# Scores of 16 small heads: four-pass float32 matmuls against halves stacked by DMA for single-pass matmuls

## The reference, cut to what matters

```
def mha(q_in, k_in, v_in, ...):
    Q = (q_in @ qw + qb).reshape(Bq, Lq, 16, 8)
    K = (k_in @ kw + kb).reshape(Bq, Lk, 16, 8)
    V = (v_in @ vw + vb).reshape(Bq, Lk, 16, 8)
    scores = jnp.einsum('bqhd,bkhd->bhqk', Q, K) / np.sqrt(8)
    attn = jax.nn.softmax(scores, axis=-1)
    out = jnp.einsum('bhqk,bkhd->bqhd', attn, V).reshape(Bq, Lq, 128)
    return out @ ow + ob
```

## Time and profile before

| | |
|---|---|
| time, median of 3 | 1052.72 us (1051.87 to 1052.78) |
| span of the profiled execution, first to last instruction | 1049.9 us |
| what lies around that span, against the median | 2.8 us |
| granted TensorE clock, mean over the span | 0.990 |
| TensorE (PE) busy | 1008.1 us, 96% |
| VectorE (DVE) busy | 748.8 us, 71% |
| GpSimd (POOL) busy | 686.9 us, 65% |
| ScalarE (ACT) busy | 607.4 us, 58% |
| DMA queues | 5.9%, 0.6% and 0.1% of 16 engines' span |

### The profile page before, as it was taken

How to read it: one execution, slowest core, us unless ns; L and a number is a source line. 1 busy time by engine, 2 the same in 40 slices (tenths; PEclk the granted TensorE clock), 3 DMA queues, 4 the chain that set the end, 5 groups by cost and what they waited for, 6 DMA issues and landing times.

```text
span 1049.9 us, 28844 instructions
## 1 busy us (share of the span) xinstructions
PE 1008.1 (96%) x11729; PEld 636.9 (61%) x11729; DVE 748.8 (71%) x1852; ACT 607.4 (58%) x898; POOL 686.9 (65%) x819
## 2 busy tenths in 40 slices
PE   7889999999999999999999999999999999999998
PEld 5345555556655776667676655665556566565576
DVE  7778888778884443776787788878888866777421
ACT  2144445577667455455554576776666677766752
POOL 6688988687986332111114699987889777688720
PEclk9699999999999999999999999999999999999999
DMA  6300000000001102000000000000000000000011
GB/s 217 122 2 2 22 12 13 20 14 23 12 22 28 36 31 99 13 7 7 8 7 19 14 8 2 2 2 2 3 1 2 2 2 2 2 2 2 1 41 41
DMA packets 9282, 22.76 MB, mean 22 GB/s; under 512 B 1392, under 2 KB 1648, under 8 KB 8768
## 3 DMA queue, kind: packets, MB, share of 16 engines
q1 hardware_dynamic: 9152, 20.94, 5.9%
HBM read 18.77 MB, written 2.15 MB: 20 GB/s over the span
## 4 chain that ended last, share of the span: by engine, by line
PE 82%; DVE 7%; POOL 5%; issue 4%; ACT 2%; DMA 0%; SPq 0%; POOLq 0%; ACTq 0%; DVEq 0%
PE weighed L708 12%; PE scores L680 11%; PE row_scores L643 7%; PE scores L906 6%; PE weighed L731 5%; PE scores L598 4%; PE quads L579 4%; DVE negmax L1226 3%; PE quads L605 3%; PE scores L693 3%; PE row_scores L906 3%; PE quads L590 3%; PE row_scores L721 2%; PE scores L721 2%; PE weighed L923 2%
## 5 line engine op out<-in xcount | busy, mean ns | idle before, releaser
L1226 DVE TENSOR_REDUCE negmax<-row_scores 128x8 f32<-128x616 f32 (+1 forms) x312 | 298.8, 958 | 100.4 <-PE row_scores L643 74.9
L1731 ACT ACTIVATE p<-scores 128x1024 f32<-128x1024 f32 (+1 forms) x253 | 250.9, 1020 | 165.6 <-PE scores L693 139.2
L680 PE MATMUL scores<-qblk,work 32*77 32x512 f32 (+1 forms) x1256 | 202.8, 612 | 6.2 <-ACT p L1731 3.3
L708 PE MATMUL weighed<-p,v 77*32 77x128 f32 (+1 forms) x5120 | 172.9, 276 | 0.1
L1906 POOL TENSOR_TENSOR qblk<-work,pack_const 128x512 f32<-128x512 f32 x160 | 166.5, 1041 | 0.0
L1916 POOL TENSOR_TENSOR kblk_r<-work,pack_const 128x308 fp32r<-128x308 f32 (+1 forms) x160 | 134.0, 838 | 44.4 <-PE row_scores L643 27.0
L643 PE MATMUL row_scores<-kblk_r,qr 32*128 32x308 f32 (+1 forms) x624 | 140.9, 443 | 13.8 <-DVE negmax L1226 12.3
L708 PEld LDWEIGHTS weighed<-p,v 77*32 77x32 f32 (+1 forms) x5120 | 130.0, 109 | 36.0 <-issue 29.4
L643 PEld LDWEIGHTS row_scores<-kblk_r,qr 32*128 32x128 f32 x624 | 61.4, 185 | 98.0 <-issue 70.9
L693 PE MATMUL scores<-nblk,select 32*77 32x512 bf16 (+1 forms) x628 | 94.8, 376 | 0.0
L1242 DVE STREAM_TRANSPOSE nat<-weighed 128x256 f32<-128x256 f32 x160 | 70.9, 443 | 32.6 <-PE weighed L708 30.7
(11 more groups left out here) (332 smaller groups left out, 1862.9 us busy)
## 6 DMA issues: line engine op xcount, KB each, us to landing
shared<-gates_hbm SPq DMA_DIRECT2D x24, 256.0 KB, 3.1
shared<-in_ctx_tok SPq DMA_DIRECT2D x15, 154.0 KB
pack_w_l<-in_w_l SPq DMA_DIRECT2D x1, 2058.5 KB, 11.5
x<-in_x_tok SPq DMA_DIRECT2D x8, 256.0 KB, 6.2
out_x<-x SPq DMA_DIRECT2D x8, 256.0 KB, 2.0
layers_w<-in_w_l SPq DMA_DIRECT2D x1, 1289.0 KB, 9.8
ctxT<-in_ctxT SPq DMA_DIRECT2D x1, 1232.0 KB, 8.9
layers_w<-in_w_ada SPq DMA_DIRECT2D x1, 582.0 KB, 5.5
```

Source lines behind the costliest of these rows:

```text
L680: mm = e.matmul(score_banks(n, g // 2)[0:nk, g % 2, :], k_of[q % 3][at, s * nk:(s + 1) * nk], qblk[n % 2][at, :], start=layer.mask != "qk" ...
L708: mm = e.matmul(av_bank[TILE * j:TILE * j + TILE, i2 * S:(i2 + 1) * S], v[0:nk, at:at + TILE], p[n % 2][0:nk, g * NJ + j, :], start=i1 == ...
L1226: e.tensor_reduce(negmax[q % 2][:, 2 * h:2 * h + 2, s * NJ:(s + 1) * NJ], row_banks(n, h)[:, :, 0:NJ * nk].rearrange("p g (j k) -> p g j k ...
L1731: e.activation(p[n % 2][0:nk, 8 * h:8 * h + 8, :], score_banks(n, h)[0:nk].rearrange("p g (j q) -> p (g j) q", j=NJ), ACT.Exp, bias=hide, ...
```

## The change

The exact scores are made otherwise. Once a quad, ScalarE rounds the keys too (`round_k`; the queries already were), and GpSimd subtracts the rounded from the exact value (`split_q`, `split_k`), so that queries and keys are there as a high and a low half. SyncE then stacks them for two jobs at a time (`stack_pair`): eight SBUF-to-SBUF DMAs put, for each head, the four products high x high, low key x high query, and so on (`PARTS`), into 32 partitions (8 dims x 4 parts), in rings of three pairs. The weights are permuted on the host (`_by_dim`), so that the heads of a group lie in every fourth partition. `exact` is now 16 matmuls of 32 rows and 128 columns, one for each head, in rounded float32; `qblk` and `spread_q` are gone. The first `exact` of a pair waits for its 8 DMAs. `q_of` and `k_of` are rings of two. In slots with 128 keys `shift(t, 1)` now follows `shift(t, 0)` directly, ahead of `quad_ahead`. SyncE's program is written in slots as well, since the loads of gates and context now stand between the stacking.

```diff
 (exact, TensorE)
-                ready, value = k_ready(q)
-                w.wait_ge(ready, value)
-                w.wait_ge(qblk_done, n + 1)
-                for g in range(NG):
-                    at = slice(TILE * g, TILE * (g + 1))
-                    mm = e.matmul(score_banks(n, g // 2)[0:nk, g % 2, :], k_of[q % 3][at, s * nk:(s + 1) * nk], qblk[n % 2][at, :],
-                                  start=layer.mask != "qk" or g >= 2, stop=False, skip_group_check=True,
-                                  tile_position=(TILE * g, 0))
+                m, half = divmod(n, 2)
+                w.wait_ge(*pair_landed(m))
+                for j in range(NJ):
+                    for g in range(NG):
+                        at = slice(TILE * g, TILE * (g + 1))
+                        mm = e.matmul(score_banks(n, g // 2)[0:nk, g % 2, j * S:(j + 1) * S],
+                                      keys_of(m, nk)[at, j, half * nk:(half + 1) * nk].bitcast(F32R),
+                                      q_ring[m % PAIRS][at, j, half * S:(half + 1) * S].bitcast(F32R),
+                                      start=j == 0 and (layer.mask != "qk" or g >= 2), stop=False, skip_group_check=True,
+                                      tile_position=(TILE * g, 0))
 (attention, TensorE)
                         exact(t)
                         shift(t, 0)
-                        if not is_wide(t):
-                            shift(t, 1)
+                        shift(t, 1)
                     if is_wide(t):
                         quad_ahead(qi, cl)
-                        shift(t, 1)
 (ScalarE)
+            def round_k(q):
+                cols = QUAD * layer_of(q).nk
+                ready, value = k_ready(q)
+                w.wait_ge(ready, value)
+                w.wait_ge(k_split, q)
+                if q:
+                    w.wait_ge(*pair_landed(2 * q - 2))
+                    w.wait_ge(*pair_landed(2 * q - 1))
+                e.copy(k_high[:, 0:cols], k_of[q % 2][:, 0:cols]).then_inc(k_rounded, 1)
...
                         exponentiate(t, 0)
                     if cl == 2 and qi + 1 in quads:
                         round_max(qi + 1)
+                    if cl == 3 and qi + 2 in quads:
+                        round_k(qi + 2)
                     if t in jobs:
                         exponentiate(t, 1)
 (GpSimd)
+            def split_q(q):
+                w.wait_ge(qr_done, q + 1)
+                if q:
+                    w.wait_ge(*pair_landed(2 * q - 2))
+                    w.wait_ge(*pair_landed(2 * q - 1))
+                e.tensor_tensor(q_low, q_of[q % 2], qr[q % 3][:, :].bitcast(F32), ALU.subtract).then_inc(q_split, 1)
...
-                    if t + 1 in jobs:
-                        spread_q(t + 1)
...
+                    if cl == 3 and qi + 2 in quads:
+                        split_q(qi + 2)
+                        split_k(qi + 2)
 (SyncE)
+            def stack_pair(m):
+                q, half = divmod(m, 2)
+                nk = layer_of(q).nk
+                q_at, k_at = (slice(2 * half * n, 2 * (half + 1) * n) for n in (S, nk))
+                w.wait_ge(q_split, q + 1)
+                w.wait_ge(k_split, q + 1)
+                w.wait_ge(scores_done, 2 * (m - PAIRS) + 2)
+                landed = pair_landed(m)[0]
+                for x, (of_q, of_k) in enumerate(PARTS):
+                    k_src = k_low if of_k else k_high[:, :].bitcast(F32)
+                    e.dma_start(keys_of(m, nk)[x:128:NJ, :, :], k_src[:, k_at]).then_inc(landed, 16)
+                for x, (of_q, of_k) in reversed(list(enumerate(PARTS))):
+                    q_src = q_low if of_q else qr[q % 3][:, :].bitcast(F32)
+                    e.dma_start(q_ring[m % PAIRS][x:128:NJ, :, :], q_src[:, q_at]).then_inc(landed, 16)
...
+            for t in range(-4, 8 * NB + TAIL):
+                if t % 2 == 0 and t + 4 < 8 * NB:
+                    stack_pair((t + 4) // 2)
```

More of the change, by code:

```diff
@@ L241, in build @@
         work = sb("work", [128, 9, QUAD * S])
-        xn, q_of, k_of = ([work[:, 3 * i + j, :] for j in range(3)] for i in range(3))
+        xn, q_of, k_of = [work[:, j, :] for j in range(3)], [work[:, 3 + j, :] for j in range(2)], [work[:, 6 + j, :] for j in range(2)]
+        q_low, k_low = work[:, 5, :], work[:, 8, :]
+        k_high = sb("k_high", [128, QUAD * S], F32R)
+        last_hidden, first_mix = sb("last_hidden", [128, QUAD * S]), sb("first_mix", [128, NE * D])
         bn = [sb(f"bn{f}", [128, QUAD, 6]) for f in range(2)]
@@ L272, in build @@
               + [p_ for p_, _ in PACKS] + [f"x{c}" for c in range(NB)]
-              + [f"g{i}" for i in range(2)] + ["ctx_first"] + [f"ctx_tok{i}" for i in range(3)]}
+              + [f"g{i}" for i in range(2)] + [f"pair{i}" for i in range(PAIRS)] + ["ctx_first"] + [f"ctx_tok{i}" for i in range(3)]}
         pack_of = {name: p_ for p_, items in PACKS for name, _ in items}
@@ L420, in mod_bank, with pair_landed, keys_of @@
             return row_scores[:, 1, :] if c < 2 else scores[:, 0, :]
+        def pair_landed(m):
+            return ld[f"pair{m % PAIRS}"], 16 * 2 * len(PARTS) * (m // PAIRS + 1)
+        def keys_of(m, nk):
+            return k_ring[m % PAIRS].rearrange("p j k -> p (j k)")[:, 0:NJ * 2 * nk].rearrange("p (j k) -> p j k", j=NJ)
         def q_ready(q):
@@ L504, in build @@
         evT = attnT
-        hidden = [[work[:, k, :] for k in range(7)], [quad(normT, 2 + k) for k in range(6)] + [qblk[0][:, :]]]
+        hidden = [[work[:, k, :] for k in range(7)], [quad(normT, 2 + k) for k in range(6)] + [last_hidden[:, :]]]
         gate_z = four(1, 1)
         gate_sig = [rot[0][:, :] if c == NB - 1 else four(1, 2 + c % 2) for c in range(NB)]
-        mix_in = [qblk[1][:, 0:NE * D], four(1, 0)[:, 0:NE * D]]
+        mix_in = [first_mix[:, :], four(1, 0)[:, 0:NE * D]]
         mix_step = nat
@@ L1201, in rotate @@
                 w.wait_ge(*freed)
+                if which:
+                    w.wait_ge(kblk_r_done, 4 * (q - 2) + 4)
                 e.tensor_tensor(by_seq(dst), by_seq(bank),
@@ L1204, in rotate @@
                 w.wait_ge(rope_done, 2 * (q - 1) + which + 1)
-                e.stream_shuffle(rot[which][:, :], bank, [i ^ (HD // 2) for i in range(TILE)]).then_inc(rope_half, 1)
+                e.stream_shuffle(rot[which][:, :], bank, [i ^ (NJ * HD // 2) for i in range(TILE)]).then_inc(rope_half, 1)
                 if not rope_by_pool(q, which):
@@ L2093, in sync_program, with load_gate @@
             w.wait_ge(gates_stored, 16)
-            for k, (_, g, c) in enumerate(GATE_USES):
+            def load_gate(k):
+                _, g, c = GATE_USES[k]
                 if k >= 2:
@@ L2098, in sync_program, with load_context @@
                     [128, QUAD, D])).then_inc(ld[f"g{k % 2}"], 16)
-            w.wait_ge(mlp_delta, NB)
-            for use in range(1, 2 * NB):
-                if use == 3:
-                    for name in LATE:
-                        e.dma_start(packs[name], a[name]).then_inc(ld[name], 16)
+            def load_context(use):
                 if use >= 4:
```

91 lines of the change are left out of this document (57 added, 34 removed).

## The result

The changed kernel takes 1066.8 us (median of four runs, 1059.5 to 1069.7) against 1052.75 us: a ratio of 1.0127 [1.0088, 1.0166]. It is slower by 1.3%, where 1042.5 us was forecast and 1058 us was the upper end. The profiled execution has a span of 1061.8 us, 11.9 us more than before. (Some executions of the experiments e1 and e4 were disturbed, among them the profiled ones: their ratios leave these out, and of their traces only what lies ahead of 612 us is read.)

The account below looks back on a forecast made before the run. Most slots were taken as bound by `rows`, VectorE's maximum and PSUM release, with TensorE's work as long. Terms -(4.4 + 4.2 + 3.6) + 1 + 1 = -10.2 us gave 1042.5 us, range 1032 to 1058.

Parts of the forecast that it names:

- the slot: Most slots: `rows`, VectorE's maximum and PSUM release set the 1.39 us between `rows`, so shorter exact scores leave it unchanged.
- the large rival (997 us): TensorE is the bound after all: 0.3 to 0.4 us off each of 160 slots, 997 us; larger gain's chance 0.14.
- 0.65 us for exact behind `rows`: New exact scores where `rows(t+5, 1)` goes ahead: 0.65 us (0.5 to 0.97) instead of 0.92 with 77 keys.
- loads and streams in series: Rival: weight loads and streams add up, or single passes aren't shorter; 1048 to 1054 us, chance 0.18.
- the gains: Slots with `project_out` and l0 save 4.4 us, slots waiting for ScalarE 4.2, last six jobs of each phase 3.6.
- work taken from TensorE was priced at zero: Most slots: TensorE reaches the wait for the maximum 0.3 us earlier and stands idle there; 0 us.
- the deadline of `round_k`: Next quad's `round_k`: a pair's stacking lands 8.2 us after exact against 9.0 allowed; covered, +1 us (-1 to +6).
- The forecast's own sign of being wrong: Changed profile: TensorE, ScalarE or GpSimd waiting for the stacking DMAs would show the forecast wrong.
- SyncE's issues set the pace: Rival: 16 stacking issues a quad bind from 0.95 us each; 1060 us at 1 us; slower through DMA or ScalarE 0.18.
- the moved shift: `shift(t, 1)` moved beside `shift(t, 0)`: the same matmuls, 0 us.
- GpSimd's relief: GpSimd: `spread_q` (166.5 us) goes, splits (some 75 us) come, releasing nothing late in the chain; 0 us.
- the partial form of the first rival: TensorE partly the bound: 0.1 us saved in each slot, 1042 - 14 = 1028 us.

Follow-up runs that it names:

- e1: Changed kernel with two matmuls that add zero between `shift(t, 0)` and `shift(t, 1)` of every attention slot; 1082 us, ratio 1.0285.
- e4: Changed kernel with `shift(t, 1)` put back behind `quad_ahead` in slots with 128 keys; 1062.4 us, ratio 1.0095.
- e14: Changed kernel with second buffers for `k_high`, `k_low` and `q_low`, and four-pass exact scores in 28 of 160 slots; 1040.9 us, ratio 0.9892.
- e2: Kernel before with exact scores in one F32R pass, no stacking, DMAs or new waits; 1058.5 us, ratio 1.0073.
- e7: Changed kernel with four-pass exact scores in slots 0 to 7 only; 1063.9 us, ratio 1.0115.
- e9: Changed kernel with a second buffer for each of `k_high`, `k_low` and `q_low`, single-pass exact kept; 1057.75 us, ratio 1.0055.
- e5: Changed kernel with four-pass fp32 exact scores over the same stacked tiles, all else kept; 1072.3 us, ratio 1.0202.
- e10: Changed kernel with second buffers for `k_high`, `k_low` and `q_low`, and four-pass exact scores everywhere; 1059.3 us, ratio 1.0066.
- e3: Changed kernel with stacking transfers for the first three pairs only, later waits satisfied by those; 1055.9 us, ratio 1.0056.

## Why the prediction was wrong

**Right: the slot.** Exact to shift fell to 0.33 us, `rows(t+6, 0)` kept its 1.40 us and the release its 0.15, TensorE's share went to 91% and GpSimd's busy time to 616.5 us. The maximum does set the slot, and the large rival (997 us) fell. One detail was mis-sized: I took 0.65 us for exact behind `rows`, with 0.5 as the lower end, and it is 0.33 with 77 keys (16 matmuls, 0.08 us a round); with 128 keys it is 0.50.

The rival "loads and streams in series" fell too: a load takes 167 ns in the mean (below) and a round 0.08 to 0.13 us, so the loads overlap although each round uses the row groups of the one before.

```profile
L695 PEld LDWEIGHTS scores<-q_ring,k_ring 32*77 32x77 f32 (+1 forms) x2512 | 100.0, 167 | 7.9 <-ACT shared L1695 1.9
```

By the Trainium skill, "TensorE: Matmul & The Clock Gate", section "The mechanism", loads overlap matmuls in flight only between different row groups; this trace, with its rounds shorter than a load, doesn't bear that out.

**Right: the gains.** They come through wherever the clock stays up. In the changed kernel the l0 quads give 1.3 us from slot 12 to 28 (0.33 us a quad, 0.3 forecast), l3s gives 2.3 us from slot 100 to 128 (0.33 a quad, 0.25 forecast). In e14 the time from slot 56 to slot 64 gives 3.3 us and slots 148 to the last another 3.3 us. Its span is 1038.7 us; the forecast was 1039.7. The size of the sum was right for a kernel whose clock stays and whose rounding doesn't wait, but that the two agree to 1 us is partly luck: e14 keeps the old length in 28 slots, and slots 64 to 76 give it 3.4 us where the forecast had a loss of 1.

**Wrong, the missed step: work taken from TensorE was priced at zero.** The forecast put 0.3 us of new idle time into most slots and wrote "0 us" behind it. It listed the busy share of 90% and did not ask what clock TensorE would be granted at it. No rival had it, and the range had nothing for it. e2 shows the step alone: work taken away and nothing added, 6 us slower. Against the gain of about 10 us that was forecast, it is a cost of some 16 us (an estimate: 6 + 10). In the changed kernel the largest part lies in the start (7 us at slot 32, by e7 beside it), the rest in the ends of the phases and slots 92 to 96. The Trainium skill tells of the kind of thing in "TensorE: Matmul & The Clock Gate", section "HAM oscillation — how this bites in real kernels": matmul bursts with DMA waits between them keep falling to the half rate. The fall at 616.2, behind a late landing, agrees. The other falls add that idle times of 0.4 to 1.1 us inside a slot, with no DMA in them, stand ahead of a fall too, and the start adds that the half rate can last through 22 us in which TensorE is shown busy.

**Wrong, the mis-sized term: the deadline of `round_k`.** It was put at 8.2 us against 9.0, "covered, by 0.8 us". The forecast's own sign of being wrong, ScalarE or GpSimd waiting for the stacking DMAs, came. Its parts were right: 0.65 us an issue, and a landing of 2.1 us where 3.1 was taken. But it counted one pair. Both pairs of a quad are issued back to back, behind the splits, so the chain is splits (2.1 us), 16 issues (10.9), landing (1.6): 14.7 us in a quad of 15.3. A slack of 0.6 us per quad is lost at the first disturbance and isn't won back. This is nearly the rival "SyncE's issues set the pace", at 1060 us, which was tied to slower issues; the issues were as fast as in the earlier trace rows, and what closed the loop was single buffers. Its price, from e9 beside the changed kernel, is 9 us, where the term was +1 (-1 to +6); at a like clock it is some 2 us, within the term's range, and the rest goes with the clock. With four passes, and hardly a difference in clock, it is 13 us (e5 beside e10).

**Right at nothing:** the moved shift (e4), the transfers as traffic (e9 beside e3). **Not quite nothing:** GpSimd's relief. e10 has no shorter exact scores, and yet it gains 2.0 us on the kernel before from slot 64 to 76. There TensorE had waited for GpSimd's `xh` (0.9 and 0.5 us), and in e10 these two waits are gone:

```profile
PE scores L557 <- POOL xh L1936: 0.9, 1, 0.9
PE quads L557 <- POOL xh L1936: 0.5, 1, 0.5
```

A slip with no effect on the forecast: the partial form of the first rival, 0.1 us in each of 160 slots, is 16 us and not 14.

So 1042.5 + 16 + 9 is 1067.5; 1066.8 was measured. That is no independent check: 1042.5 + 16 is the time of e2 by construction, and the sum only says that e2 and e9 take nearly the same time (1058.5 and 1057.75). Nor is it a split into clock and loop, since most of the 9 us goes with the clock as well.

## What to carry to other kernels

When a change takes work from TensorE in slots that something else bounds, that work may have held its clock: write down, for each slot, what idle time the change makes, and give the lower clock a case in the range. If the saving is real, keep some of the old work in the few slots where the clock would fall (starts, ends, changes of layer). And for each tile that a transfer reads, walk the whole loop (produce, issue all that is queued, land, overwrite) against the period, not the one transfer against its deadline; a second buffer for three tiles (2 KB in each partition for each) came with 9 us less in the single-pass kernel and 13 us less in the four-pass one. And list the clock beside each time: two kernels at different mean clocks differ by that first.

## What the runs showed of the hardware

- TensorE's clock fell to 1.2 GHz at 90.6 us behind idle times no longer than 1.11 us, and stayed there for 3.3 us; the longest stretch, from 25 us on, was 48 us in the changed kernel, the last 22 of them with TensorE shown busy for 97%.
- Four-pass exact scores in the first slots brought the clock back by 54.6 us in each of ten traces; single-pass ones left it low until between 62.9 and 73.4 us in each of six. At 1.2 GHz the four 128-column fp32 matmuls of L613 took 2.07 us in place of 1.16.
- Sixteen single-pass matmuls of 128 columns with weights of their own, four row groups abreast: 0.33 us to the next group with 77 keys, 0.50 us with 128.
- A transfer from SBUF to SBUF of 128 KB whose rows go to every fourth partition: 0.65 us of SyncE's queue, 2.1 us from issue to landing. 640 of them (some with 77 keys are smaller), 27% of the DMA engines' time, had no effect on the kernel's time that could be measured (e9 beside e3):

```profile
q_ring<-work SPq DMA_DIRECT2D x160, 128.0 KB, 2.1
```

- With matmuls that add nothing in every slot, the clock stayed at 1.00 from 75 to 612 us (e1), where the changed kernel fell three times; it didn't come back earlier in the start for them.
